# Inverse norms copied to features as three bf16 pieces in one product, with Newton's last step on VectorE and the orders of the local layers written anew

## What is computed

```
q = l2norm(q) * qs                      # q / max(|q|, 1e-12), per token and head
k = l2norm(k) * ksc
q = q * cos * scale + rotate_half(q) * sin * scale
k = k * cos * inv + rotate_half(k) * sin * inv
sim = einsum(q, k of two windows of 32) * 8; masked; softmax; times v; times Wo
```

## Time and profile before

| | |
|---|---|
| median of 3 runs | 4070.32 us (4061.17 to 4073.91) |
| the profiled execution's own time | 4063.49 us |
| its span in the profile | 4061.4 us |
| TensorE busy | 3807.5 us, 94% of the span |
| VectorE busy | 3026.9 us, 75% |
| ScalarE busy | 2350.1 us, 58% |
| GpSimd busy | 2311.4 us, 57% |

### The profile page before, as it was taken

The page is one execution under the profiler, slowest core; times in us unless marked ns, Lnnn a source line. Parts: engine busy times, 40 slices in busy tenths (PEclk is TensorE's granted clock), DMA queues, the critical chain, the costliest instruction groups (busy, mean ns, idle before and its releaser), DMA issues.

```text
span 4061.4 us, 162148 instructions
## 1 busy us (share of the span) xinstructions
PE 3807.5 (94%) x72308; PEld 2145.7 (53%) x72308; DVE 3026.9 (75%) x3509; ACT 2350.1 (58%) x2850; POOL 2311.4 (57%) x1892
## 2 busy tenths in 40 slices
PE   7999999779999999999999999999899999999996
PEld 3555555445555555554555555555555555555553
DVE  6878777667777777776777777777777777777774
ACT  4555565546565656565656565565566566656553
POOL 3554454366565656665666656665556565666661
PEclk9999999889999999999999999999999999999998
DMA  1000000144444444443444444444444444454442
GB/s 54 4 4 4 4 4 4 38 103 98 108 98 105 102 113 108 110 107 90 107 114 100 104 97 113 107 104 98 101 114 98 106 99 105 104 115 96 110 103 80
DMA packets 162062, 348.69 MB, mean 86 GB/s; under 512 B 32606, under 2 KB 41948, under 8 KB 155100
## 3 DMA queue, kind: packets, MB, share of 16 engines
q1 hardware_dynamic: 161372, 338.32, 35.7%
HBM read 24.24 MB, written 4.19 MB: 7 GB/s over the span
## 4 chain that ended last, share of the span: by engine, by line
PE 45%; issue 2%; DMA 2%; DVE 2%; ACT 1%; SPq 1%; ACTq 0%; DVEq 0%
PE psB L632 22%; PE psA L632 17%; DMA vev<-vo 2%; PE psB L710 2%; PE psA L684 2%; PE psB L684 1%; ACT pb L937 1%; PE psA L710 1%; SPq L452 1%; SPq L468 0%; DMA kf<-h 0%; SPq L470 0%; DVE h L1163 0%; DVE wvtl L1115 0%; DVE ts L1155 0%
## 5 line engine op out<-in xcount | busy, mean ns | idle before, releaser
L1263 POOL TENSOR_TENSOR sq<-sq 128x512 f32<-128x512 f32 x384 | 490.2, 1295 | 469.5 <-ACT sq L907 468.9
L1258 POOL TENSOR_TENSOR h<-h,ts 128x512 f32<-128x512 f32 x384 | 489.9, 1276 | 210.5 <-DVE ts L1155 210.5
L1239 POOL TENSOR_TENSOR pt<-wk,pt 128x1024 f16<-128x1024 f32 (+3 forms) x256 | 367.7, 1454 | 399.8 <-DVE pt L1096 322.1
L1259 POOL TENSOR_TENSOR h<-h,ts 128x512 f32<-128x512 f32 x384 | 490.6, 1277 | 0.0
L907 ACT ACTIVATE sq<-psA 128x1024 f32<-128x1024 f32 x240 | 245.8, 1024 | 168.1 <-PE psA L632 168.1
L1147 DVE TENSOR_TENSOR h<-psA,t_rot 128x1024 f32<-128x1024 f32 x240 | 293.0, 1221 | 46.0 <-ACT sq L907 20.3
L632 PE MATMUL psB<-vev,ptb 64*32 64x65 f32 x9216 | 244.5, 225 | 55.9 <-ACT pb L937 36.9
L1155 DVE TENSOR_TENSOR ts<-psA,t_rot 128x1024 f32<-128x1024 f32 x240 | 291.4, 1214 | 3.1 <-POOL h L1259 3.1
L632 PEld LDWEIGHTS psB<-vev,ptb 64*32 64x32 f32 x9216 | 194.4, 106 | 173.1 <-issue 98.4
L1273 POOL TENSOR_SCALAR f_a<-f_a 128x512 f32<-128x512 f32 x48 | 31.2, 650 | 404.5 <-DVE f_a L1203 404.5
L1163 DVE TENSOR_TENSOR h<-h,psB 128x1024 f32<-128x1024 f32 x192 | 229.5, 1217 | 42.3 <-PE psB L632 40.2
(11 more groups left out here) (332 smaller groups left out, 10640.6 us busy)
## 6 DMA issues: line engine op xcount, KB each, us to landing
qf<-h SPq DMA_DIRECT2D x768, 136.0 KB
kf<-h SPq DMA_DIRECT2D x768, 136.0 KB
vev<-vo SPq DMA_DIRECT2D x192, 260.0 KB, 4.1
vev<-vo SPq DMA_DIRECT2D x192, 227.5 KB, 4.5
stage<-wqk SPq DMA_DIRECT2D x12, 512.0 KB, 4.8
...
```

The lines of the kernel that those rows point to most:

```text
L1239: e.tensor_tensor(pt[g][pr][:, :, 1, o:o + w], wk[(slot_of(s)[0] - 1) % SLOTS][:, :, 0:w], pt[g][pr][:, :, 0, o:o + w], ALU.subtract).then ...
L1258: e.tensor_tensor(halves_of(h, 0), halves_of(h, 0), t[1], ALU.subtract)
L1259: e.tensor_tensor(halves_of(h, 1), halves_of(h, 1), t[0], ALU.add).then_inc(ended["ad"])
L1263: e.tensor_tensor(sqb[c][:, 0, :], sqb[c][:, 0, :], sqb[c][:, 1, :], ALU.add).then_inc(ended["qa"])
```

## The change

`bc` takes a bf16 matrix and a bf16 tile `n_p` in place of the f32 ones. The eight rows that hold one sum now hold three different pieces of it. `spread` has a -1 in three of the eight rows (pieces 0, 1 and 2) and adds them up in one product of 32 rows. To make the pieces, two ScalarE steps `na` and `nc` round `n_a` to bf16 in `n_h` (which shares the memory of `n_r`), and two VectorE steps `nb` and `nd` subtract what is rounded from the rows of the later pieces, through the per-row factors `later` and `last` (0 or -1). `nw` moves from GpSimd to VectorE, where it is two instructions and gives the negative of the inverse norm. Only `nd` waits for the products `bc` of the half before. All five lists are written in a new order.

```
-    spread = (q % W == k // W) * 1.0
+    piece = p % W // 4
+    spread = ((p % 4)[:, None] == p[None, :] // W) & (piece < 3)[:, None]
+    masks = np.concatenate([maskaq, maskak, np.eye(128), lmask, -1.0 * spread], 1)
+    pieces = np.stack([-1.0 * (piece > 0), -1.0 * (piece > 1)], 1)
...
 TENSOR = (
-    "vp00:A ot00:B pj10:A pj11:B sc100:B tp01:A sc101 sc102 sc103 pj13:A pj12:A ng10 pv011:B pv010:B ss1:B "
-    "sc110:A tp10:B sc111 sc112 ot01:B sc113 f1:A ng11 pv100:B f2:B f0:B pv101:A bc11:A vp10:B bc10:A tp11:B "
...
+    "lb:B pv010:A pj11:A sc100:B pj13:B sc101 sc102 sc103 pj12:A sc110:A ng10 sc111 sc112 sc113 tp10:B ot01:B "
+    "ng11 ss1:B pv101:A tp11:A pv100:B pj01:B+1 vp10:A ot10:B pv110:A vp11:A pv111:B f1:A bc10:B f2:A vp01:B+1 "
+    "bc11:A pj00:B+1 pj02:A+1 ot11:B pj03:A+1 f0:B op:B ss0:B+1 fo:A sc000:A+1 sc001+1 sc002+1 sc003+1 pj10:A+1 "
+    "vp00:B+1 ng00+1 sc010:B+1 sc011+1 sc012+1 tp00:A+1 sc013+1 la:A+1 bc00:B+1 pv001:A+1 ng01+1 pv000:A+1 "
...
 SCALAR = (
+    "ex00 nc0 wh0 ve00 te00 lq lw ex01 te01 oe00 lr sq11 sq13 sq12 ex10 te10 oe01 ex11 nr1 ns1 sq01+1 te11 ve10 "
+    "oe10 na1 ve11 nc1 wh1 ge1 ge2 ve01+1 sq00+1 oe11 sq03+1 sq02+1 xh+1 ge0 nr0+1 ns0+1 sq10+1 oh tb1+1 na0+1 "
 VECTOR = (
+    "nm001 nm000 bm01 bm02 bm03 nm011 ol00 ln nm010 tc11 ts11 mx10 tc13 ts13 mx11 tc12 ts12 ol01 nm101 nm100 nw1 "
+    "tc01+1 ts01+1 nm110 nb1 ol10 nd1 nm111 bm10 bm11 fm1 fm2 bm12 bm13 tc00+1 ts00+1 ol11 tc02+1 tc03+1 fm0 "
+    "ts03+1 wl1 ts02+1 rs fr mx00+1 nw0+1 tc10+1 nb0+1 ts10+1 nd0+1 wl0+1 ow mx01+1 bm00+1 "
 GPSIMD = (
+    "qa00 qa01 ad00 qa03 qa02 ad02 xl ad03 qa10 qa11 ad10 ad11 qa12 qa13 ad13 lx ad01+1 ad12 "
...
         t_masks = sb("t_masks", [128, 384 + NT * 2 * W + 128], BF16)
         spread = t_masks[:, 384 + NT * 2 * W:]
+        n_p = sb("n_p", [128, S], BF16)
+        n_h = n_r[:, 0:S // 2].bitcast(BF16)
...
                 elif kind == "bc":
-                    e.wait_ge(*done("nw", v))
+                    e.wait_ge(*done("nd", v))
-                        p = mm(o[:, 512 * x:512 * x + 512], spread[rows, :], n_a[rows, :], tile_position=(64 * k + 32 * x, 0))
+                        p = mm(o[:, 512 * x:512 * x + 512], spread[rows, :], n_p[rows, :], tile_position=(64 * k + 32 * x, 0))
...
                     if v:
-                        e.wait_ge(*all_done("bc", (v - 1, 0), (v - 1, 1)))
+                        e.wait_ge(*done("nd", v - 1))
                     e.activation(n_a[:, :], n_r[:, :], ACT.Square, scale=0.5 ** 0.5).then_inc(ended["ns"])
+                elif kind in ("na", "nc"):
+                    e.wait_ge(*done("nw" if kind == "na" else "nb", v))
+                    e.activation(n_h[:, :], n_a[:, :], ACT.Copy).then_inc(ended[kind])
...
+                elif kind == "nw":
+                    e.wait_ge(*done("ns", v))
+                    e.tensor_tensor(n_a[:, :], n_s[:, :], n_a[:, :], ALU.mult).then_inc(s_nwh)
+                    e.wait_ge(s_nwh, count[s])
+                    e.scalar_tensor_tensor(out=n_a[:, :], in0=n_a[:, :], scalar=-1.5, in1=n_r[:, :], op0=ALU.add, op1=ALU.mult
+                                           ).then_inc(ended["nw"])
+                elif kind == "nb":
+                    e.wait_ge(*done("na", v))
+                    e.scalar_tensor_tensor(out=n_a[:, :], in0=n_h[:, :], scalar=later, in1=n_a[:, :], op0=ALU.mult, op1=ALU.add
+                                           ).then_inc(ended["nb"])
+                elif kind == "nd":
+                    e.wait_ge(*done("nc", v))
+                    if v:
+                        e.wait_ge(*all_done("bc", (v - 1, 0), (v - 1, 1)))
+                    e.scalar_tensor_tensor(out=n_p[:, :], in0=n_h[:, :], scalar=last, in1=n_a[:, :], op0=ALU.mult, op1=ALU.add
+                                           ).then_inc(ended["nd"])
...
-                elif kind == "nw":
-                    e.wait_ge(*done("ns", v))
-                    e.tensor_tensor(n_a[:, :], n_s[:, :], n_a[:, :], ALU.mult).then_inc(s_nwh)
-                    e.wait_ge(s_nwh, 2 * count[s] - 1)
-                    e.tensor_scalar(n_a[:, :], n_a[:, :], -1.0, 1.5, ALU.mult, ALU.add).then_inc(s_nwh)
-                    e.wait_ge(s_nwh, 2 * count[s])
-                    e.tensor_tensor(n_a[:, :], n_a[:, :], n_r[:, :], ALU.mult).then_inc(ended["nw"])
```

More of the change, by code:

```diff
@@ L62, in constants @@
     maskak = np.where(k >= q, 0.0, NEG)
-    masks = np.concatenate([maskaq, maskak, np.eye(128), lmask], 1)
+    piece = p % W // 4
+    spread = ((p % 4)[:, None] == p[None, :] // W) & (piece < 3)[:, None]
+    masks = np.concatenate([maskaq, maskak, np.eye(128), lmask, -1.0 * spread], 1)
     heads = (q // W == np.arange(W)[None, :] % 4) * 1.0
-    spread = (q % W == k // W) * 1.0
-    mats = np.concatenate([np.eye(128), np.eye(128) - 1.0 / 128, np.full((128, 128), 1.0 / 128), spread, heads], 1)
+    pieces = np.stack([-1.0 * (piece > 0), -1.0 * (piece > 1)], 1)
+    mats = np.concatenate([np.eye(128), np.eye(128) - 1.0 / 128, np.full((128, 128), 1.0 / 128), heads, pieces], 1)
     return {"tab": tab.reshape(128, 4 * S).astype(f), "masks": masks.astype(f), "left": left.reshape(128, 256),
@@ L239, in flat @@
             return t.rearrange("p a b -> p (a b)")
-        t_mats = sb("t_mats", [128, 384 + 160])
-        ident, center, mean, spread, heads = (t_mats[:, a:z] for a, z in ((0, 128), (128, 256), (256, 384), (384, 512),
-                                                                           (512, 544)))
-        t_masks = sb("t_masks", [128, 384 + NT * 2 * W], BF16)
+        t_mats = sb("t_mats", [128, 384 + 34])
+        ident, center, mean, heads = (t_mats[:, a:z] for a, z in ((0, 128), (128, 256), (256, 384), (384, 416)))
+        later, last = t_mats[:, 416:417], t_mats[:, 417:418]
+        t_masks = sb("t_masks", [128, 384 + NT * 2 * W + 128], BF16)
+        spread = t_masks[:, 384 + NT * 2 * W:]
         maskaq, maskak, identb = (t_masks[:, 128 * n:128 * n + 128] for n in range(3))
@@ L270, in program @@
         wbig = flat(ot[0])[:, 0:3 * 1024]
-        st_masks, st_left, t_wmod = (flat(ot[1])[:, a:z] for a, z in ((0, 640), (640, 896), (896, 1664)))
+        st_masks, st_left, t_wmod = (flat(ot[1])[:, a:z] for a, z in ((0, 768), (768, 1024), (1024, 1792)))
         acc = [sb(f"acc{n}", [128, S], F32, early) for n in range(2)]
@@ L341, in program @@
             "sc", "mx", "ng", "ex", "tp", "te", "pv", "nm", "ot", "oe", "op", "rs", "pj", "sq", "tc", "ts", "ad", "ss", "nr",
[L342 removed]
+            "ns", "nw", "na", "nb", "nc", "nd", "xh", "xl", "wh", "wl", "tb", "oh", "ow", "ol", "qa", "bc", "bm", "vp", "ve", "vd", "la", "lq", "lw", "lb", "lr", "ln", "lx", "f", "ge", "fm", "fo", "fr")}
         s_nsl, s_nsr, s_nwh, s_lrl, s_lrr, s_lxh, s_rc, s_init, s_w1s = (
```

10 lines of the change are left out of this document (2 added, 8 removed), and 7 rows, old and new, of tables (TENSOR, VECTOR).

## The result

| | before | changed |
|---|---|---|
| median | 4067.84 us (4 runs, 4061.17 to 4073.91) | 4171.4 us (4 runs, 4156.93 to 4177.42) |
| ratio, 95% interval | | 1.025 (1.0215 to 1.0284) |
| the profiled execution | 4063.49 us | 4156.93 us |

The changed kernel is slower by about 104 us. I had forecast 3960 us and faster.

What follows compares the result with a forecast made beforehand. TensorE, busy 94% of the span, was taken as the bound. From 4063.5 us, minus 142 (product) plus 36 (late `bc`) gave 3957.5, put at 3960 us for the runs' higher median; 8-in-10 range 3900 to 4030 us.

Steps and rivals of the forecast that it cites:

- The product: TensorE's `bc` steps: 0.74 us less for each of 192 steps, 142 us saved.
- The idle time of 2.8 us a round: TensorE's idle time in the local layers, 127.6 us in 3050 us; the forecast left it unchanged.
- The late `bc`: TensorE waits for the norm's longer path over ScalarE and VectorE: 0.75 us per round, 36 us lost.
- the room of 0.4: Second half of a round: TensorE's 11.2 us between `ss1` and `bc10` against 10.8 us on ScalarE and VectorE.
- Waits for GpSimd: New VectorE instructions beside a working GpSimd: 0.37 us of waiting each, bringing VectorE to 59.3 us a round.
- VectorE as the bound, 4197 us: Rival: each of eight new VectorE instructions held 1.27 us by GpSimd, rounds of 69.5 us, kernel slower; chance 0.08.
- The new order: Rewritten lists: only the path from `ss` to `bc` was costed, 36 us lost; TensorE's other idle time left unchanged.
- The clock: TensorE's granted clock over the local layers, 0.99 (the 2.4 GHz level): no gain in reach.
- The rest … I count 0.: Mask table grows by 128 columns once, no DMA of the loop changes in size: counted 0.

Runs made afterwards that it cites:

- run 8: Kernel before, old orders, with one bf16 piece rounded on ScalarE into `n_p`, Newton's step on GpSimd, nothing added on VectorE: 4010.5 us, 0.9855 of the kernel before.
- run 10: Changed kernel with two bf16 pieces in place of three: `nc` and `nd` gone, `nb` writes `n_p`; 4101.6 us, 1.0083 of the kernel before.
- Run 2: Kernel before's f32 products and Newton's step on GpSimd, put in the changed kernel's new orders: 4194.3 us, 1.0297 of the kernel before.
- Run 3: Changed kernel with `bm01` moved ahead of `nm001` and `nm000` on VectorE: 4132.1 us, 1.0146 of the kernel before.
- run 11: Changed kernel with TensorE's `tp10` between `sc112` and `sc113`, and `ss1` ahead of `ng11`: 4191.7 us, 1.0302 of the kernel before.

## Why the prediction was wrong

- **The product** (192 x 0.74 = 142 us). Right in itself: 0.32 us a step, and 140 us from start to start over the 186 steps of the 47 rounds. The step that failed is the sentence before it, "a microsecond taken from TensorE is a microsecond of time, as long as no other engine makes TensorE wait for it". The condition did not hold. In run 8, with one added rounding on ScalarE and nothing on VectorE, 63 us of it reach the time. The idle time of 2.8 us a round was no proof of slack in the other loops. That these are nearly as long as TensorE's own is what I take from it; which of them holds it, no run shows.
- **The late `bc`** (36 us, 0.75 us per round). Near, 44 us, but with a wrong share. It falls wholly on the second half of a round (43 waits of 1.0 us); the first half, which I had not added up, has none. There I had 2 x 0.37 us for `nb1` and `nd1`. They lose 0.33 and 1.09 us, and 1.42 less the room of 0.4 is the 1.0 us of the wait. Its removal (run 10) is worth 70 us, more than the wait itself; where the other 26 us come from, I have not shown.
- **Waits for GpSimd** (0.37 us for each new instruction). Too high as a mean, 0.19 us, and too low for the one that `bc10` waits for, `nd1`. What I had said of their places was right, `nb1` and `nd1` meet `ad` and `nw` does not. The Trainium skill's rule that the loser waits out the other's instruction (page "SBUF — State Buffer", section "Who interferes with whom") shows in the 1.84 us of `nd1`, which is GpSimd's 1.26 us at the same time and its own 0.7, less 0.1.
- **VectorE as the bound, 4197 us**. The sign and nearly the time came true, by luck, for the mechanism did not: VectorE is busy 56 us of 68, below my 59.3. Its price was to be 1.27 us for each instruction, and it is 0.19 in the mean.
- **The new order.** Here the forecast failed most. Of five rewritten lists I looked at the path of the norm and left the rest at "The other idle time of TensorE (2.8 us per round) I leave as it is". Run 2 prices that at 121 us. Two things were in the lists and the rows. `bm01`, ahead of two `nm` before and behind them now, starts a path of four DMA issues and a landing (3.67 us), for which `sc100` waits (psB, 25 us); with the waits on psA it is 60 us more of waiting for keys. Run 3, which undoes this one step, is worth 39 us. And score steps with almost nothing between them, above all `sc110` to `sc113`, draw instructions faster than these come: +84 us at boundaries (33.5 to 117.7), of which 53 are inside score steps on psA (7 to 60). For the list this is shown in part only: run 11, which loosens it in one place, brings 17 us of the 84 back. Such gaps stood in the trace of before too, as "issue" inside score and `pv` steps; I had counted them as part of 2.8 us that nobody would change.
- **The clock** ("no clock gain is in reach"). I had asked only for a gain. Its loss is 22 to 34 us (estimated above), and it comes with the orders: run 2 alone has 147 us at 1.2 GHz against 37.5.
- **"The rest … I count 0."** The size of the loop's DMAs is the same, as said; their time of issue is not, and the waits for keys show what that costs.

The sum over the 47 rounds: -139 (product), +165 (idle), +22 to +34 (clock), +35 to +23 of busy time that I cannot place, together +83 us, the difference of the two stretches. Some 10 us more lie ahead of the first `rs` (923.05 against 912.80).
